# Two residual graph layers in one kernel: v with both halves of its weight side by side, VectorE's dependent steps set apart, q and k rounded on GpSimd, new orders

## The reference

```python
def layer0(x, mask):                       # masked attention
    v = relu(x @ Wv + bv); q = relu(x @ Wq + bq); k = relu(x @ Wk + bk)
    att = softmax((q @ k.T) * mask - 9e15 * (1 - mask), axis=-1)
    return relu((att @ v) @ Wo + bo)

def layer1(x, mask):                       # weighted mean over the neighbours
    h = x @ W_w.T + W_b
    e, f = h @ a_w[:128], h @ a_w[128:]
    u = mask * exp(e[:, None] + f[None, :] + a_b)
    return (u / u.sum(-1, keepdims=True)) @ h

x = layernorm(x + layer0(x, adj))
x = layernorm(x + layer1(x, adj))
```

## Time and profile before

| | us |
|---|---|
| median of 3 runs (lowest, highest) | 408.95 (407.3, 409.02) |
| the profiled execution, its own time | 411.1 |
| its span, first to last instruction | 408.4 |
| TensorE busy | 393.6, 2860 matmuls |
| VectorE busy | 339.3, 1000 instructions |
| ScalarE busy | 336.5, 646 instructions |
| GpSimd busy | 264.7, 230 instructions |
| bytes moved | 80.71 MB, mean 198 GB/s |

### The profile page before, as it was taken

One profiled execution on the slowest core, in us unless ns is written; L12 is line 12 of the kernel. 1 busy time (PEld: TensorE's weight loads), 2 busy tenths in 40 slices (PEclk: granted clock), 3 DMA queues, 4 the chain that ended last, 5 costly groups with the idle time before them and its releaser, 6 DMA issues.

```text
span 408.4 us, 8871 instructions
## 1 busy us (share of the span) xinstructions
PE 393.6 (96%) x2860; PEld 366.9 (90%) x2860; DVE 339.3 (83%) x1000; ACT 336.5 (82%) x646; POOL 264.7 (65%) x230
## 2 busy tenths in 40 slices
PE   8999999999999999999999999999999999999990
PEld 8899988999999989999999999999999998899990
DVE  3886898889689995999969997799969999979665
ACT  4877778997799877899689988898879988998743
POOL 1563735467529596496947879196974986683672
PEclk9999999999999999999999999999999999999997
DMA  7593636166570676716883547908367269697011
GB/s 249 210 323 114 219 119 240 70 228 225 198 273 8 233 276 203 270 54 207 301 281 140 188 175 249 336 36 282 142 246 260 80 233 313 238 345 238 3 51 51
DMA packets 37868, 80.71 MB, mean 198 GB/s; under 512 B 2752, under 2 KB 19264, under 8 KB 37824
## 3 DMA queue, kind: packets, MB, share of 16 engines
q1 hardware_dynamic: 37680, 80.03, 56.1%
q10 hardware_dynamic: 144, 0.14, 0.2%
HBM read 75.96 MB, written 4.19 MB: 196 GB/s over the span
## 4 chain that ended last, share of the span: by engine, by line
PE 75%; DVE 8%; ACT 6%; issue 5%; POOL 3%; DMA 3%; SPq 0%; ACTq 0%; DVEq 0%; POOLq 0%
PE m_ps L1606 12%; PE pt_ps L1558 11%; PE av_ps L1570 6%; PE s_ps L1499 6%; PE av_ps L1571 6%; PE av_ps L1572 6%; PE s_ps L1501 6%; PE s_ps L1500 6%; PE m_ps L1499 3%; PE m_ps L1500 3%; PE m_ps L1501 3%; PE m_ps L1506 3%; DMA adjt_in<-in_adj_t_dram 3%; DVE prob L970 1%; ACT prob L622 1%
## 5 line engine op out<-in xcount | busy, mean ns | idle before, releaser
L978 DVE TENSOR_TENSOR prob_tl<-pt_ps,prob_th 128x512 fp32r<-128x512 f32 x128 | 85.9, 683 | 20.6 <-ACT prob_th L630 20.1
L630 ACT ACTIVATE prob_th<-pt_ps 128x512 fp32r<-128x512 f32 x128 | 74.3, 592 | 29.3 <-PE pt_ps L1558 28.6
L970 DVE CUSTOM_DVE_ANT_0 prob<-s_ps,penalty 128x1024 f32<-128x1024 f32 x64 | 78.1, 1220 | 9.3 <-PE pt_ps L1558 4.5
L622 ACT ACTIVATE prob<-prob,neg_max 128x1024 f32<-128x1024 f32 x64 | 73.5, 1148 | 5.1 <-DVE neg_max L970 5.0
L1570 PE MATMUL av_ps<-prob_th,vh 128*128 128x256 f32 x256 | 74.5, 291 | 0.0
L389 POOL TENSOR_SCALAR penalty<-raw 128x1024 bf16<-128x1024 f32 x64 | 66.5, 1053 | 12.1 <-DMA raw<-in_adj_dram 8.3
L1558 PE MATMUL pt_ps<-rhs,prob 128*128 128x128 f32 x512 | 74.0, 273 | 0.0
L1572 PE MATMUL av_ps<-prob_th,vl 128*128 128x256 f32 x256 | 72.4, 283 | 0.0
L1571 PE MATMUL av_ps<-prob_tl,vh 128*128 128x256 f32 x256 | 72.4, 283 | 0.0
L1558 PEld LDWEIGHTS pt_ps<-rhs,prob 128*128 128x128 f32 x512 | 59.4, 141 | 6.8 <-DVE prob_tl L978 0.3
L1606 PE MATMUL m_ps<-g,adj_t 128*128 128x258 f32 x448 | 62.5, 288 | 1.7 <-ACT raw L608 1.4
(11 more groups left out here) (156 smaller groups left out, 931.4 us busy)
## 6 DMA issues: line engine op xcount, KB each, us to landing
raw<-in_adj_dram SPq DMA_DIRECT2D x64, 512.0 KB, 5.2
adjt_in<-in_adj_t_dram SPq DMA_DIRECT2D x56, 512.0 KB, 4.6
raw<-in_x_t_dram SPq DMA_DIRECT2D x16, 256.0 KB, 3.6
x_in<-in_x_dram SPq DMA_DIRECT2D x8, 512.0 KB, 4.7
raw<-in_adj_t_dram SPq DMA_DIRECT2D x8, 512.0 KB, 5.7
out_dram<-out_sb SPq DMA_DIRECT2D x14, 256.0 KB, 5.4
out_dram<-out_sb SPq DMA_DIRECT2D x4, 128.0 KB, 1.8
wb<-in_pack_b_dram SPq DMA_DIRECT2D x1, 320.0 KB, 4.0
```

Source lines behind the costliest of these rows:

```text
L622: sc.activation(prob[i % 2][:, :], prob[i % 2][:, :], ACT.Exp, bias=neg_max[:, i:i + 1], scale=-1.0, accum_out=row_sum[b % 2][:, i:i + 1]) ...
L630: sc.activation(prob_th[n % 2][:, tiles(k), (i % 2) * P:(i % 2 + 1) * P], pt_ps[k][:, :].rearrange("p (c n) -> p c n", n=P), ACT.Copy).the ...
L970: v.tensor_tensor_reduce(out=prob[i % 2][:, :], in0=s_ps[:, :, :].rearrange("p a n -> p (a n)"), in1=penalty[:, n % RING, :], scale=-1.0, ...
L978: v.tensor_tensor(prob_tl[n % 2][at], pt_ps[k][:, :].rearrange("p (c n) -> p c n", n=P), prob_th[n % 2][at].bitcast(F32), ALU.subtract).th ...
```

## The change

v's weight halves go side by side: a v slot now holds two tiles (`project_v(b, j)`, j = 0 to 3), VectorE adds the bias to column b (`v_bias`) and column b to column a (`v_sum`), ScalarE takes the relu (`v_relu`). bv no longer goes through the output's bias. `o_out` becomes `inverse_sum`, `o_bias` and `o_sum`, `stats` is cut in two (`stats0`/`mean_var0`, `stats1`/`mean_var1`) and `scale_out` in three, each piece with its own place in VectorE's list, and v_low and o_low have two buffers. From batch 1 on GpSimd rounds q and k (`q_hi`, `k_hi`). The last pair of x1 and of the output is normalised by VectorE (`norm0_end`, `norm1_end`). A pass has 30 uses of the three banks instead of 28. All lists are reordered; the diff shows those of which the prediction speaks.

```diff
-            def project_v(b, k):
+            def project_v(b, j):
...
-                for c in range(TH):
-                    t = k * TH + c
-                    last = product(blk(vv, c), (blk(xth, t), blk(xtl, t)), (wvh, wvl))
+                for c in range(2):
+                    t = 2 * j + c
+                    last = product_side_by_side(vv[:, c * PAIR:(c + 1) * PAIR], (blk(xth, t), blk(xtl, t)), flat(w_hl[:, 2, :, :]), D)
                 last.then_inc(v_full, 1)
...
-            def v_out(b, k):
-                wait(dve, vl_done, 2 * (b - 1) + k + 1)
-                dve.wait_ge(v_full, 2 * b + k + 1)
-                v.tensor_tensor(half(vf, k).rearrange("p (t d) -> p t d", d=D),
-                                bank["v", b, k][:, :].rearrange("p (t d) -> p t d", d=D),
-                                rows(minus_bv[:, :], TH), ALU.max).then_inc(v_evac, 1)
+            def v_bias(b, j):
...
+                wait(dve, v_summed, TH * b + j - 1)
+                dve.wait_ge(v_full, TH * b + j + 1)
+                vv = bank["v", b, j][:, :].rearrange("p (t a d) -> p t a d", a=2, d=D)
+                v.tensor_tensor(v_low[j % 2][:, :, :], vv[:, :, 1, :], rows(bv_row, 2), ALU.add).then_inc(v_biased, 1)
+
+            def v_sum(b, j):
+                dve.wait_ge(v_biased, TH * b + j + 1)
+                vv = bank["v", b, j][:, :].rearrange("p (t a d) -> p t a d", a=2, d=D)
+                v.tensor_tensor(vv[:, :, 0, :], vv[:, :, 0, :], v_low[j % 2][:, :, :], ALU.add).then_inc(v_summed, 1)
...
+            def v_relu(b, j):
+                wait(act, vl_done, 2 * (b - 1) + j // 2 + 1)
+                act.wait_ge(v_summed, TH * b + j + 1)
+                vv = bank["v", b, j][:, :].rearrange("p (t a d) -> p t a d", a=2, d=D)
+                sc.activation(vf[:, j * PAIR:(j + 1) * PAIR].rearrange("p (t d) -> p t d", d=D), vv[:, :, 0, :],
+                              ACT.Relu).then_inc(v_evac, 1)
...
+            def q_hi(b, k):
+                wait(pool, s_full, T * (b - 1) + TH * (k + 1))
+                pool.wait_ge(q_evac, 2 * b + k + 1)
+                gp.tensor_copy(half(qh, k), half(qf, k)).then_inc(qh_done[1], 1)
...
+            def k_hi(b, k):
+                wait(pool, s_full, T * b)
+                pool.wait_ge(k_evac, 2 * b + k + 1)
+                gp.tensor_copy(half(kh, k), half(kf, k)).then_inc(kh_done[1], 1)
...
-                pe.matmul(av_ps[:, 2 * E1:2 * E1 + D], bv_wide[:, :], raw_o, start=True, stop=True).then_inc(set_full, 1)
...
+            def norm0_end():
+                dve.wait_ge(rstd0_done, B + TH - 1)
+                for t in range(T - 2, T):
+                    v.tensor_scalar(x1[:, t, :], x1[:, t, :], mv0[:, t, 0:1], rstd0[:, t:t + 1],
+                                    ALU.subtract, ALU.mult).then_inc(x1_end, 1)
+
+            def norm1_end():
+                dve.wait_ge(out_free[1], 16 * LAST)
+                dve.wait_ge(rstd1_done, B + TH - 1)
+                for t in range(T - 2, T):
+                    v.tensor_scalar(out_sb[:, t, :], gs[:, t, 0:D], mv1[:, t, 0:1], rstd1[:, t:t + 1],
+                                    ALU.subtract, ALU.mult).then_inc(out_end, 1)
```

More of the change, by code:

```diff
@@ L1286, in batch_pass @@
+                v_bias(p + 1, 1)
                 prob_lo(p, 2, 1)
                 if there(p - 2):
-                    agg_out(p - 2, 4)
+                    den_out(p - 2)
                 prob_lo(p, 3, 0)
                 if there(p - 2):
-                    agg_out(p - 2, 5)
-                if there(p - 2):
-                    agg_out(p - 2, 6)
-                prob_lo(p, 3, 1)
-                x1_lo(p - 1, 0)
-                mask_max(p, 5)
-                if there(p - 2):
-                    agg_out(p - 2, 7)
+                    inv_den_out(p - 2)
@@ L1299, in batch_pass @@
+                v_sum(p + 1, 1)
                 if there(p - 2):
                     scale_out(p - 2)
+                x1_lo(p - 1, 0)
+                prob_lo(p, 3, 1)
+                mask_max(p, 5)
+                av_lo(p, 0)
                 h_out(p - 1, 0)
+                prob_lo(p, 4, 0)
                 h_out(p - 1, 1)
-                av_lo(p, 0)
-                prob_lo(p, 4, 0)
+                if there(p - 2):
+                    stats1(p - 2, 0)
+                mask_max(p, 6)
@@ L1312, in batch_pass @@
+                prob_lo(p, 5, 0)
+                inverse_sum(p, 1)
+                h_out(p - 1, 7)
+                prob_lo(p, 5, 1)
+                v_bias(p + 1, 2)
                 av_lo(p, 1)
-                h_out(p - 1, 4)
-                prob_lo(p, 5, 0)
-                prob_lo(p, 5, 1)
-                h_out(p - 1, 5)
                 mask_max(p, 7)
-                h_out(p - 1, 6)
-                o_out(p, 0)
-                v_out(p + 1, 1)
+                v_sum(p + 1, 2)
+                if there(p - 2):
+                    mean_var1(p - 2, 1)
@@ L1346, in tail @@
-                agg_out(LAST - 2, 1)
-                mask_max(LAST, 2)
-                stats0(LAST - 1, 1)
-                agg_out(LAST - 2, 2)
-                var_eps0(LAST - 1)
+                o_bias(LAST - 1, 1)
+                o_sum(LAST - 1, 1)
+                residual0(LAST - 1, 1)
+                o_bias(LAST - 1, 2)
+                stats0(LAST - 1, 0)
+                o_sum(LAST - 1, 2)
+                residual0(LAST - 1, 2)
+                mean_var0(LAST - 1, 0)
+                av_lo(LAST - 1, 3)
@@ new lines, in tail @@
+                mask_max(LAST, 1)
+                o_bias(LAST - 1, 3)
+                agg_out(LAST - 2, 0)
+                agg_out(LAST - 2, 1)
+                o_sum(LAST - 1, 3)
+                residual0(LAST - 1, 3)
+                prob_lo(LAST, 0, 0)
+                stats0(LAST - 1, 1)
+                mean_var0(LAST - 1, 1)
+                var_eps0(LAST - 1)
+                mask_max(LAST, 2)
+                agg_out(LAST - 2, 2)
+                prob_lo(LAST, 0, 1)
+                shift_mean0(LAST - 1)
```

881 lines of the change are left out of this document (464 added, 417 removed), and 9 rows, old and new, of tables (HEAD_SLOTS, PASS_SLOTS).

## The result

The changed kernel takes **402.62 us** (median of 4 runs, 401.91 to 404.75) beside 408.6 us of the kernel before in the same session (median of 4, 407.3 to 409.02). The ratio is **0.9857** (95% interval 0.9815 to 0.9900): 6 us faster, where 8.4 were forecast. The profiled execution took 401.9 us for a span of 400.2.

The account below looks back on a forecast made before the run. TensorE's own issue was taken to bound each pass. Terms: v -6.3, head +0.7, end -2.8, together -8.4 us, from a median of 408.95 to 400.6 us; 8-in-10 range 396.5 to 408.

Parts of the forecast that it names:

- v side by side: TensorE's v projection, batches 1 to 7: 0.45 us a slot, 0.90 a half against 1.37, saving 6.3 us (5.2 to 8.0).
- VectorE's queue: nothing: VectorE's added steps, +1.4 us a pass, and split dependent steps counted at nothing, covered by 5.6 us not busy a pass.
- ScalarE and GpSimd: Rounding copies of q and k moved from ScalarE to GpSimd, +2.4 us a pass on GpSimd; no cost to the kernel.
- c: Time of one GpSimd rounding copy of 128x512: taken as 0.6 us, between 0.53 and 1.3.
- the chain: GpSimd's steps behind a pass's last scores that ready q and k for the next scores: 5.1 us with 0.6 a copy.
- TensorE's stretch: TensorE's work between a pass's last scores and the next batch's first scores: 5.9 us, less some 0.25 for signals.
- the room: Time to spare for GpSimd's rounding and subtracting before the next batch's first scores: 0.5 us.
- its load falls, off the path: ScalarE loses four 128x512 copies a pass and gets four half-size v_relu; this was said to lie off the path.
- The head, +0.7: Start and batch 0: two v slots come behind the first scores, +0.9 us; two bv matmuls go, -0.2 us.
- Carried-over waits, 0 (+-2.5): TensorE's waits, some 1 us in an earlier pass, taken as unchanged; between 2.5 us less and 2.5 us more.
- The end, -2.8: Earlier last-pair transposes -1.6 us, a residual pair moved -0.5, last normalisation on VectorE -0.7; range -0.8 to -3.8.
- the bank of a v slot: Rival, chance 0.10: v banks freed too late; 0.3 us a slot takes the whole gain, 0.4 gives 412 us.

Follow-up runs that it names:

- the second execution: The kernel before, unaltered, profiled a second time: 408.25 us, span 406.5.
- adjacent: The changed kernel with VectorE's dependent steps next to each other again in the passes, same instructions: 408.69 us, ratio 0.9997 to the kernel before.
- agg_first: The changed kernel with one VectorE step moved, an aggregate's reduction ahead of four mean-and-variance instructions: 402.61 us, ratio 0.9831 to the kernel before.
- kh_twice: The changed kernel with each rounding copy of k (batches 1 to 7) made twice on GpSimd: 412.47 us, ratio 1.0083 to the kernel before.
- the first execution: The kernel before, unaltered, in its first profiled execution: 411.1 us, span 408.4.
- v_alone_on_before: The kernel before with v side by side alone, both slots of a half standing together: 464.12 us, ratio 1.1349 to the kernel before.
- v_spread_on_before: The kernel before with v side by side, the two slots of a half set apart: 425.17 us, ratio 1.0410 to the kernel before.

## Why the forecast was right, and by how much it was off

- **v side by side, -6.3 forecast.** The form is what the price said: the 28 slots of batches 1 to 7 take 13.88 us, of which 1.3 are the five waits, so 0.45 a slot. Before, the 14 halves took 18.63 us in the second execution, 1.33 each, not 1.37: I had taken one half's row for all, and the other half of a pass takes 1.28. Without the waits that is -6.05, with them -4.75. The mis-sized term is the wait, 1.3 us: I had looked for it at ScalarE's end of the bank chain, and it sits at VectorE's reduction.
- **"VectorE's queue: nothing", the step that failed as an argument.** I let 5.6 us of free time in a pass stand for cover. The free time is not where the short steps are: one reduction 0.74 us late costs 0.64 us a pass (adjacent), and 0.37 us of mean-and-variance in front of another cost 0.25 (agg_first). In these lists the splitting is not a gift beside the gain: without it a pass gives back nearly all of its 0.68 us. Whether moving that one reduction alone would do as well was not tried.
- **ScalarE and GpSimd.** c was 0.61 to 0.62 (0.6 taken), the chain 5.05 us (5.1), TensorE's stretch 5.76 (5.9), the room 0.5 (0.5); kh_twice shows that this room is real. But "its load falls, off the path" was wrong: with the copies on ScalarE, placed as before, a pass is 1.03 us longer. The term was nothing in my sum because I compared the new chain only with its deadline and not with the old chain under the new load.
- **The head, +0.7.** Start and batch 0 together are +1.05. But the four slots of batch 1 stand in batch 0 and save 1.01 us there, which v's term already has; the head by itself costs 2.06, three times what I had. The two slots behind scores(0,0) take 0.68 and 0.60 us to the next start (0.45 each taken), and TensorE has waits in batch 0 where the second execution of before has none. The longest is for VectorE's mask_max:

```profile
24.15 0.47 PE L1607 MATMUL s_ps<-kh,qh 128*128 128x512 f32 x1 [0.36 <-DVE neg_max L997]
```

The start itself can come at 11.3 or at 12.2, for a reason I had not seen (last section); in the old kernel it was 12.22 and 11.46.
- **Carried-over waits, 0 (+-2.5).** Outside v's slots passes 1 to 6 are 1.1 us shorter than in the second execution, 0.8 of it in passes 2 and 3. The 2.15 us by which the first execution lay over the median were mostly waits of passes 2 and 3 (1.8 us between the two executions), so that taking them off had already taken these waits out.
- **The end, -2.8.** -1.7 or -2.5 by the execution of before. Of it the last tile's normalisation 0.57 (0.7 forecast, with 0.45 for a pair that takes 0.60), from the last matmul to it 0.36 for the moved residual (0.5). The transposes came 1.5 or 2.4 us earlier by the orders, and nothing of that by VectorE's normalisation.

Forecast 8.4, measured 6.3 between the spans and 6.0 between the medians. The misses of the terms are v +1.55, the head +1.36 and the end +0.3, against -1.1 in the rest of the passes, which I had put at nothing; that the sum came within 2.1 us is in part the luck of that last term. Of the signs that I had named, v's slots, GpSimd's copies, the scores without a wait for kl and the two stretches of the end came as written; late passes of 46.65 us lie over the 46.3 to 46.5.

The terms do not add up as I had them add. From pass 1 to the end the whole change is worth 7.4 us between the profiled executions. Over the same stretch v's form undone costs 4.3 us, the splitting undone 5.6 and the rounding moved back 6.9, nearly 17 together. Each holds a different place just short of TensorE's need. Of the rivals, the bank of a v slot is real in the old orders: an aggregate waits for v_relu 3.6 us in all in v_alone_on_before and 3.0 in v_spread_on_before. The changed kernel has no such wait; its 0.25 us a pass are for another bank, that of an aggregate.

## What to carry to other kernels

Where one engine is busy in all of a stage, a part of a change is not worth its instructions but what it leaves of the slack at the nearest deadline; ask at each place who frees the bank or the buffer, what stands ahead of it on its queue, and by how many tenths of a us it is early. A new slot in a ring shifts every hand-over behind it: list the pairs anew before pricing the work. And undo the parts one at a time from the finished kernel, not only add them to the old one: both directions were needed here.
